# Flamingo cross-attention with a routed FFN: the context of batches 1 to 3 loads as 32-row blocks and is turned by VectorE

## The chip, the core and the metric

The kernel runs on one core of one Trainium2 chip. The metric is the device time of one execution in microseconds (us); three executions of the kernel before took 322.89 to 324.15, with a median of 324.1. The engines are PE (TensorE), ACT (ScalarE), DVE (VectorE), POOL (GpSimd) and SP (SyncE, which here only issues DMAs); "PEld" rows are weight loads of TensorE.

## The reference, cut to what matters

There are 4 batches of 512 tokens with 256 features, 16 heads of 16 features, and attention windows of 64 queries that see their own and the previous 64 keys. Queries come from the normalised x, keys and values from the context.

```python
q = proj(query, W_q, b_q)          # query = layernorm(x)
k = proj(key, W_k, b_k)            # key = value = ctx_1024
v = proj(value, W_v, b_v)
x = _local_attention(q, k, v, mask)
...
x = x + jnp.tanh(g_xattn[0]) * _L0_xattn_ref(_layernorm(x, axis=-1), ctx_1024, ctx_1024, ...)
x = x + jnp.tanh(g_ffn[0]) * _L0_ffn_ref(_layernorm(x, axis=-1), ...)   # top-1 router, 16 experts
```

A projection `proj(x, W, b)` is `x @ W.T + b`, so TensorE needs the context with its features on the partitions (`ctxT`), which is why it has to be transposed.

## The kernel before

The program has an attention part, which works through the four batches one after another, and an expert part, which is the rest of the span. Each engine's order is written out by hand; engines meet only at semaphores. A loop over `b` covers batches 0 to 2; batch 3 (`LAST`) is written out behind it. Iteration `b` also prepares batch `b + 1`, and finishes the projection, the normalisation and the router of batch `b - 1`.

A batch has 16 units: a window and one half of the heads. For a unit, DVE adds the mask to the scores and keeps a minimum (`low_of`, 4 instructions with a small read each), ACT takes the exponent (`exp`, 4 instructions), DVE the reciprocal (`r_total_of`), POOL multiplies (`norm`), PE transposes (`probsT_of`, 4 transposes), and DVE (even units) or ACT (odd units) copies the result out of PSUM (`take_probsT`). `scores(b, c)` makes the scores of four units at once, into banks that `low_of` of the four units before must have read; `attend(b, c)` multiplies four units with v. `project` is the output projection, `x1_of` adds it to x, `route`, `choose`, `count` and `rank_of` are the router.

The context of batch `n` goes through four steps. SP loads it (`load_ctx`, L310) into `ctx_rows`, with token `128 t + p` on partition `p`. PE transposes it in two parts (`ctxT_of`, L1414, 4 transposes each) into the bank `ps_wide`, ACT copies each part into `ctxT` (`take_ctxT`, L696), and PE multiplies: `k_of` (L1435, twice per batch) and `v_of` (L1446). All of this for batch `b + 1` stands in iteration `b`. The bank is shared, so PE waits for ACT's first copy before it writes the second part, and for the second copy before `attend(b, 0)`. Batch 0's context is copied out of PSUM by DVE (L1154).

The order of PE in iteration `b`, from the part that the change touches, is: `v_of(b, 1)`, `ctxT_of(b+1, 0)`, `probsT_of` 4 and 5, `ctxT_of(b+1, 1)`, `xnT_of(b+1, 1)`, `scores(b, 3)`, `attend(b, 0)`, the transposes of x1 of batch `b-1`, `probsT_of` 6 and 7, `q_of(b+1, 0)`, `route(b-1)`, `k_of(b+1, 0)`, `probsT_of` 8 and 9, `attend(b, 1)`, `scores(b+1, 0)`, `probsT_of` 10 and 11 with `count(b-1)`, `project(b, 0)`, `k_of(b+1, 1)`, `q_of(b+1, 1)`. In batch 0 there is no route and no count. `k_of(b+1, 1)` waits for `rank_of`'s first step (L1091) on DVE, because the counts lie in its bank.

SP's order in iteration `b` is `load_ctx(b+1)`, the two shifted copies of v (`shift_v`, each waits for DVE's `take_v`), then loads of the first experts' weights and a store.

Of the kernel before, what the change touches and what calls it, by code (L numbers as in the profile page):

```python
# [27 lines left out]
P = 128  # L28
# [15 lines left out]
def flamingo_kernel(nc, x, ctx_in, mask, g_xattn, g_ffn, W_q, b_q, W_k, b_k, W_v, b_v, W_o, b_o,  # L44
# [25 lines left out]
    with es:  # L70
# [44 lines left out]
        x_all = sb("x_all", [P, B, T, D])  # L115
        ctx_rows = sb("ctx_rows", [P, T, D])
        xn = sb("xn", [P, T, D])
# [93 lines left out]
        xnT_ready, xnT_taken = sem("xnT_ready"), sem("xnT_taken")  # L211
        ctxT_ready, ctxT_taken = sem("ctxT_ready"), sem("ctxT_taken")
        q_ready, q_taken = sem("q_ready"), sem("q_taken")
# [91 lines left out]
        @block.sync  # L305
        def _(sp):
            def load_ctx(n):
                if n > 0:
                    sp.wait_ge(ctxT_ready, value(n - 1, 2, 2))
                sp.dma_start(ctx_rows[:], ctx_in[n].rearrange("(t p) d -> p t d", p=P)).then_inc(ctx_in_s, 16)  # L310

# [35 lines left out]
            load_x(0, T // 2, T, x_in_late)  # L347
            load_ctx(0)
            for i, b in enumerate((b_q, b_k)):
# [11 lines left out]
            for n in range(2, B):  # L361
                load_x(n, 0, T, x_in[n])

            for b in range(B):
                if b < LAST:
                    load_ctx(b + 1)
                shift_v(b, 0)
                if b == LAST:

                    for sent in scattered:  # L370
                        sp.wait_ge(sent, 16 * T)
                    load_rows(0, 0)
                shift_v(b, 1)
                if b == 0:
                    sp.wait_ge(empty_ready, 2)
                    sp.dma_start(queue.rearrange("(s p) c -> p s c", p=P),
                                 empty_row[:].unsqueeze(1).to_broadcast([P, E * CAP // P, ROW])).then_inc(prefilled, 16)
                if 1 <= b <= 2:
                    load_w1(b - 1, b - 1)
                    load_w2(b - 1, b - 1)  # L380
                if b > 0:
                    store_x1(b - 1)
            store_x1(LAST)

# [276 lines left out]
        def _(act):  # L661
# [27 lines left out]

            def take_ctxT(n, k, ps):  # L690
                if not 0 <= n < B:
                    return
                act.wait_ge(ctxT_ready, value(n, 2, k + 1))

                act.wait_ge(v_ready, value(n - 1, 2, 2))
                act.activation(ctxT[:, k], ps[:], ACT.Copy).then_inc(ctxT_taken, 1)  # L696

            def take_k(n, g, ps):
# [94 lines left out]
            for b in range(LAST):  # L793
# [16 lines left out]
                exp(b, 8)  # L810
                take_ctxT(b + 1, 0, ps_wide)
                exp(b, 9)
                take_ctxT(b + 1, 1, ps_wide)
                take_probsT(b, 5)
# [84 lines left out]
        def _(dve):  # L899
# [14 lines left out]
            def x_norm(n):  # L914
# [5 lines left out]
                for t in range(T):  # L920
                    last = dve.tensor_scalar(xn[:, t], x_all[:, n, t], mean_var[:, n, t, 0:1], rstd[:, n, t:t + 1],
                                             ALU.subtract, ALU.mult)
                last.then_inc(xn_ready, 1)

            def mask_set_of(n):
# [246 lines left out]
            for b in range(LAST):  # L1172
# [26 lines left out]
                r_total_of(b, 8)  # L1199
                take_probsT(b, 4)  # L1200
                low_of(b, 12)
                low_of(b, 13)
# [179 lines left out]
        def _(pe):  # L1382
# [4 lines left out]
            def wT_of(i, ps):  # L1387
                pe.wait_ge(w_in[i], 16)
                for k in range(KD):
                    for d in range(KD):  # L1390
                        last = pe.transpose(ps[:, k * D + d * P:k * D + (d + 1) * P],
                                            w_raw[:, i, d, k * P:(k + 1) * P], ident[:])
                last.then_inc(wT_ready, 1)
# [14 lines left out]

            def ctxT_of(n, k, ps):
                if not 0 <= n < B:  # L1410
                    return
                pe.wait_ge(ctx_in_s, 16 * (n + 1))
                for t in range(T):
                    last = pe.transpose(ps[:, t * P:(t + 1) * P], ctx_rows[:, t, k * P:(k + 1) * P], ident[:])  # L1414
                last.then_inc(ctxT_ready, 1)
# [175 lines left out]
            for k in range(KD):  # L1591
                ctxT_of(0, k, bank[k])
            keep_warm(bank[3], 3)
# [11 lines left out]
            for b in range(LAST):  # L1605
# [27 lines left out]
                pe.wait_ge(xnT_taken, value(b + 1, 2, 1))  # L1633
                v_of(b, 1, ps_misc)
                if first:
# [12 lines left out]
                attend(b, 0)  # L1648
# [237 lines left out]
```

## Time and profile before

| what | value |
| --- | --- |
| median of three runs | 324.1 us (322.89 to 324.15) |
| the profiled execution, its own time | 324.57 us |
| its span in the profile | 322.8 us |
| PE, DVE, ACT, POOL busy over the span | 93%, 61%, 55%, 51% |
| granted TensorE clock | 1.00 in all of the span |

A page of the profile shows one execution. Its times are from the span's start. "Busy" of an engine is the union of its instructions; durations of neighbours on DVE and ACT overlap a little, so the distance between two starts is what an instruction costs its engine. In a timeline the brackets at the end of a row tell how long the engine stood idle before it, and who ended that. The busy shares over the span mix two parts: the attention part ends near 168 us, and in the expert part ACT and DVE have little to do.

### The profile page before, as it was taken

How to read it: one execution, taken by the hardware profiler on the slowest of the kernel's cores; microseconds unless marked ns; L12 is line 12 of the kernel's file. 1: busy time of each engine (PE TensorE's matmuls, PEld its weight loads, DVE VectorE, ACT ScalarE, POOL GpSimd, SP SyncE). 2: the span in 40 equal slices, each digit the busy share in tenths (PEclk: the TensorE clock that was granted, in tenths of full speed). 3: DMA queues.
4: the chain of work that ended last, by engine and by line, in shares of the span. 5: the costliest groups of instructions: out<-in, count | busy, mean ns of one | idle time of the engine just before them, and what ended most of it. 6: DMA issues, size and time to landing. Idle time of an engine off the chain costs nothing.

```text
span 322.8 us, 8448 instructions
## 1 busy us (share of the span) xinstructions
PE 299.0 (93%) x2759; PEld 244.6 (76%) x2760; DVE 195.5 (61%) x950; ACT 177.0 (55%) x666; POOL 165.3 (51%) x200
## 2 busy tenths in 40 slices
PE   7868779999999999999897999999999999999994
PEld 3437646887768866777776889898998989898974
DVE  2788898898989879899974232423425161515133
ACT  3379999999999999999754111111110202111110
POOL 6469747789769984989856122131313121121322
PEclk9999999999999999999999999999999999999999
DMA  7921299017512280230324679697979897998900
GB/s 216 288 87 25 61 376 316 7 26 229 197 60 91 58 312 3 87 93 6 95 80 185 164 215 369 201 363 235 367 212 372 238 347 257 306 310 253 365 18 13
DMA packets 48471, 60.55 MB, mean 188 GB/s; under 512 B 14712, under 2 KB 41360, under 8 KB 46384
## 3 DMA queue, kind: packets, MB, share of 16 engines
q1 hardware_dynamic: 44976, 53.20, 51.5%
q0 software_dynamic: 2560, 6.25, 5.3%
q10 hardware_dynamic: 896, 0.61, 0.6%
q8 instruction: 20, 0.33, 0.4%
q14 instruction: 19, 0.16, 0.2%
HBM read 44.60 MB, written 14.19 MB: 182 GB/s over the span
## 4 chain that ended last, share of the span: by engine, by line
PE 58%; ACT 26%; DVE 8%; issue 4%; DMA 1%; POOL 1%; SPq 0%; DVEq 0%; POOLq 0%; ACTq 0%
PE bank L1763 20%; ACT probs L712 18%; PE bank L1788 16%; PE bank L1813 5%; PE bank L1424 3%; ACT probsT L725 3%; DVE probs L958 3%; ACT q_par L686 2%; PE bank L1435 2%; PE bank L1566 1%; DMA x_all<-in_x_dram 1%; PE bank L1774 1%; PE bank L1477 1%; PE bank L1499 1%; PE bank L1537 1%
## 5 line engine op out<-in xcount | busy, mean ns | idle before, releaser
L712 ACT ACTIVATE probs<-probs,low 128x128 f32<-128x128 f32 x256 | 99.4, 407 | 2.2 <-DVE low L958 2.2
L533 POOL TENSOR_TENSOR probs<-probs,r_total 128x512 f32<-128x512 f32 x64 | 66.3, 1046 | 18.1 <-DVE r_total L967 17.6
L1763 PEld LDWEIGHTS bank<-xdT,w 128*128 128x128 f32 x480 | 66.6, 190 | 1.9 <-issue 1.2
L1763 PE MATMUL bank<-xdT,w 128*128 128x160 f32 x480 | 68.0, 300 | 0.0
L958 DVE CUSTOM_DVE_ANT_0 probs<-bank,mask_now 128x128 f32<-128x128 f32 x256 | 57.2, 283 | 6.4 <-PE bank L1465 6.0
L712 ACT ACTIVATION_READ_ACCUMULATOR probs<-probs,low 128x1 f32 x256 | 53.2, 208 | 0.0
L882 ACT ACTIVATE w_raw<-bank 128x480 f32<-128x480 f32 (+1 forms) x24 | 12.4, 526 | 62.7 <-PE bank L1763 35.7
L637 POOL DMA_INDIRECT out_dram<-base,place x16 | 14.0, 874 | 59.2 <-DVE base L1323 37.4
L646 POOL DMA_INDIRECT out_dram<-base,place x16 | 15.7, 979 | 53.7 <-DVE place L1316 43.3
L882 ACT ACTIVATE x_all<-bank 128x480 f32<-128x480 f32 (+1 forms) x24 | 12.6, 526 | 52.2 <-PE bank L1763 32.6
L1333 DVE SCALAR_TENSOR_TENSOR base<-bank,base 128x256 f32<-128x256 f32 x15 | 7.2, 482 | 51.8 <-PE bank L1788 51.8
L1477 PE MATMUL bank<-ident,probs 128*128 128x128 f32 x256 | 35.8, 276 | 2.2 <-DVE probsT L977 1.8
L1323 DVE SCALAR_TENSOR_TENSOR base<-bank,base 32x256 f32<-32x256 f32 x64 | 30.6, 477 | 9.5 <-PE bank L1813 7.6
L1477 PEld LDWEIGHTS bank<-ident,probs 128*128 128x128 f32 x256 | 28.8, 141 | 8.6 <-issue 5.6
L1788 PE MATMUL bank<-w,w_raw 128*128 128x256 f32 x128 | 29.0, 380 | 0.0
L1291 DVE STREAM_TRANSPOSE xdT<-q_blocks 128x320 f32<-128x320 f32 x16 | 8.2, 511 | 32.3 <-DMA q_blocks<-expert_queue 23.5
L1788 PEld LDWEIGHTS bank<-w,w_raw 128*128 128x128 f32 x128 | 23.9, 190 | 3.1 <-issue 0.2
L1788 PE MATMUL bank<-w,x_all 128*128 128x256 f32 x112 | 25.9, 385 | 0.0
L1465 PE MATMUL bank<-kT,q_par 32*128 32x128 f32 x512 | 18.8, 283 | 6.9 <-ACT q_par L686 3.4
L1788 PEld LDWEIGHTS bank<-w,x_all 128*128 128x128 f32 x112 | 20.7, 190 | 5.0 <-issue 2.5
L1465 PEld LDWEIGHTS bank<-kT,q_par 32*128 32x128 f32 x512 | 15.9, 186 | 10.7 <-issue 6.1
L560 POOL DMA_INDIRECT expert_queue<-rows,slot x16 | 16.6, 1036 | 11.4 <-issue 6.9
(147 smaller groups left out, 494.3 us busy)
## 6 DMA issues: line engine op xcount, KB each, us to landing
w<-in_L_ffn_w_dram SPq DMA_DIRECT2D x32, 1024.0 KB, 8.4
expert_queue<-empty_row SPq DMA_DIRECT2D x1, 5140.0 KB, 17.8
q_blocks<-expert_queue SPq DMA_DIRECT2D x62, 40.0 KB
base<-expert_queue SPq DMA_DIRECT2D x16, 129.0 KB
ctx_rows<-in_ctx_dram SPq DMA_DIRECT2D x4, 512.0 KB, 9.3
out_dram<-rows SPq DMA_DIRECT2D x4, 512.0 KB, 6.3
x_all<-in_x_dram SPq DMA_DIRECT2D x3, 512.0 KB, 7.7
v_shift<-v SPq DMA_DIRECT2D x12, 128.0 KB, 2.3
```

What stands on the lines that cost most here:

```text
L533: pool.tensor_tensor(probs[:, i % NP_], probs[:, i % NP_], r_total[:, i % NP_].unsqueeze(2).to_broadcast([P, PAIRS, 2 * WINDOW]), ALU.mult ...
L560: pool.indirect_dma_start(out=queue, out_offset=bass.IndirectOffsetOnAxis(ap=slot[n % 2][:, t:t + 1], axis=0), in_=rows[n % 2][:, t, :], i ...
L646: pool.indirect_dma_start(out=out_rows, out_offset=bass.IndirectOffsetOnAxis(ap=place[i][:, 0:1], axis=0), in_=base[i][:, 0, 0:D], in_offs ...
L712: last = act.activation(probs[:, i % NP_, j], probs[:, i % NP_, j], ACT.Exp, scale=-1.0, bias=low[:, i % NP_, j:j + 1], accum_out=total[:, ...
L882: act.activation(hidden[i][:, ms[0]:ms[-1] + 1, :], ps_hidden[m][:, 0:n].rearrange("p (m c) -> p m c", c=CAP), ACT.Gelu_apprx_tanh).then_i ...
L958: last = dve.tensor_tensor_reduce(probs[:, i % NP_, j], ps_scores[j][:, i % 4 * P:(i % 4 + 1) * P], mask_now[:, w % 2, w // 2], 1.0, 3.0e3 ...
L1323: dve.scalar_tensor_tensor(rest[:, 0:D], ps_rest[i % 2][j * REST:(j + 1) * REST, 0:D], rest[:, D:D + 1], rest[:, 0:D], ALU.mult, ALU.add). ...
L1465: last = pe.matmul(ps_scores[j][:, wi * P:(wi + 1) * P], q_par[rows_j, g, w].rearrange("p e q -> p (e q)"), kT[rows_j, g, w * WINDOW:w * W ...
L1477: last = pe.transpose(ps_probsT[i % 2][:, j * P:(j + 1) * P], probs[:, i % NP_, j], ident[:])
L1763: last = pe.matmul(ps_hidden[m][:, c * CAP:(c + 1) * CAP], w1_sb[i % 2][:, k, f * P:(f + 1) * P], xdT[i % 2][:, k], start=(k == 0), stop=( ...
L1788: last = pe.matmul(ps_y[:, 0:D], hidden[i % 2][:, k, 0:P], w2_sb[i % 2][:, k], start=(k == 0), stop=(k == KF - 1))
L1813: last = pe.matmul(ps_rest[i % 2][j * REST:(j + 1) * REST, 0:D], hidden[i % 2][:, k, P:CAP], w2_sb[i % 2][:, k], start=(step == 0), stop=( ...
```

## The change

From batch 1 on the context is loaded as 32-row blocks: token `32 s + r` lies on partition `32 j + r` for each quarter `j` of the features, with 64 features (256 bytes) in a run. One load becomes four, one for each quarter, each into 32 partitions. DVE's 32 x 32 transposes (`turn_ctx`, two per batch, 128 x 512 elements each) write `ctxT` directly. PE's 8 transposes and ACT's 2 copies per batch are gone for batches 1 to 3. Batch 0 keeps them. Since a turned block has the even features in one half of `ctxT` and the odd in the other, the transposes of W_k and W_v and those of batch 0's context read every second column.

```diff
             def load_ctx(n):
-                if n > 0:
-                    sp.wait_ge(ctxT_ready, value(n - 1, 2, 2))
-                sp.dma_start(ctx_rows[:], ctx_in[n].rearrange("(t p) d -> p t d", p=P)).then_inc(ctx_in_s, 16)
+                if not 0 <= n < B:
+                    return
+                if n == 1:
+                    sp.wait_ge(ctxT_ready, 2)
+                else:
+                    sp.wait_ge(ctxT_turned, value(n - 2, 2, 2))
+                for j in range(P // BLOCK):
+                    sp.dma_start(ctx_blocks[j * BLOCK:(j + 1) * BLOCK],
+                                 ctx_in[n, :, j * KD * BLOCK:(j + 1) * KD * BLOCK].rearrange("(s r) c -> r s c", r=BLOCK)
+                                 ).then_inc(ctx_in_s, 16)
...
-            def take_ctxT(n, k, ps):
...
-                act.activation(ctxT[:, k], ps[:], ACT.Copy).then_inc(ctxT_taken, 1)
...
-                take_ctxT(b + 1, 0, ps_wide)
                 exp(b, 9)
-                take_ctxT(b + 1, 1, ps_wide)
...
+            def turn_ctx(n, half):
+                if not 0 <= n < B:
+                    return
+                dve.wait_ge(ctx_in_s, 16 + 16 * (P // BLOCK) * n)
+
+                dve.wait_ge(v_ready, value(n - 1, 2, 2))
+                blocks = slice(half * (S // BLOCK // 2), (half + 1) * (S // BLOCK // 2))
+                dve.transpose(ctxT[:, :, half * (S // 2):(half + 1) * (S // 2)].rearrange("p k (s r) -> p s k r", r=BLOCK),
+                              ctx_blocks[:, blocks].rearrange("p s (r k) -> p s k r", k=KD)).then_inc(ctxT_turned, 1)
...
                 take_probsT(b, 4)
+                turn_ctx(b + 1, 0)
                 low_of(b, 12)
...
                 take_probsT(b, 6)
+                turn_ctx(b + 1, 1)
                 r_total_of(b, 11)
...
+                        if i in (1, 2):
+
+                            cols = w_raw[:, i, d].rearrange("p (m k) -> p k m", k=KD)[:, k]
...
             def k_of(n, g, ps):
                 if not 0 <= n < B:
                     return
-                pe.wait_ge(ctxT_taken, value(n, 2, 2))
+                if n == 0:
+                    pe.wait_ge(ctxT_taken, 2)
+                else:
+                    pe.wait_ge(ctxT_turned, value(n - 1, 2, 2))
...
-                ctxT_of(b + 1, 0, ps_wide)
-                probsT_of(b, 4)
-                probsT_of(b, 5)
-                pe.wait_ge(ctxT_taken, value(b + 1, 2, 1))
-                ctxT_of(b + 1, 1, ps_wide)
-                pe.wait_ge(v_taken, value(b, 2, 2))
-                xnT_of(b + 1, 1, ps_misc)
-                scores(b, 3)
-                pe.wait_ge(ctxT_taken, value(b + 1, 2, 2))
                 attend(b, 0)
```

On PE, in iteration 0, the stretch from `v_of(0, 1)` (which writes from `ctxT`) to `attend(0, 0)` reads before and after as follows (`ident` is the identity that makes a matmul a transpose, `probs` the softmax, `xn` the normalised x of the next batch):

```order
L1446 MATMUL bank<-wT,ctxT 128x256 x4
L1414 MATMUL bank<-ident,ctx_rows 128x128 x4
L1477 MATMUL bank<-ident,probs 128x128 x8
L1414 MATMUL bank<-ident,ctx_rows 128x128 x4
L1406 MATMUL bank<-ident,xn 128x128 x4
L1465 MATMUL bank<-kT,q_par 128x128 x16
```

```order
L1464 MATMUL bank<-wT,ctxT 128x256 x4
L1495 MATMUL bank<-ident,probs 128x128 x8
L1422 MATMUL bank<-ident,xn 128x128 x4
L1483 MATMUL bank<-kT,q_par 128x128 x16
```

The two groups of four context transposes are gone; `xnT_of` and `scores(0, 3)` stand directly behind the softmax's transposes.

On DVE, in iteration 1, behind `take_att(1, 0)`, the first fence is before and the second after (`r_total` is the reciprocal, `probsT` the copy of unit 6, `probs,low` the masked scores of unit 14):

```order
L921 TENSOR_SCALAR xn<-x_all,mean_var,rstd 128x256 x3
L967 RECIPROCAL r_total<-total 128x4 [waits exp_done]
L977 COPY probsT<-bank 128x512 [waits att_ready,probsT_ready]
L967 RECIPROCAL r_total<-total 128x4 [waits exp_done]
L958 ISA probs,low<-bank,mask_now 128x128 [waits scores_ready,probsT_ready]
```

```order
L922 TENSOR_SCALAR xn<-x_all,mean_var,rstd 128x256 x3
L978 RECIPROCAL r_total<-total 128x4 [waits exp_done]
L988 COPY probsT<-bank 128x512 [waits att_ready,probsT_ready]
L933 STREAM_TRANSPOSE ctxT<-ctx_blocks 128x8x2x32 [waits v_ready,ctx_in]
L978 RECIPROCAL r_total<-total 128x4 [waits exp_done]
L969 ISA probs,low<-bank,mask_now 128x128 [waits scores_ready,probsT_ready]
```

The second turn stands ahead of `r_total_of(1, 11)` and `low_of(1, 14)`, and everything that DVE does for the router follows it. The first turn stands in the same way between `take_probsT(b, 4)` and `low_of(b, 12)`.

On SP, the load of batch 2's context before and after (the row in front of it fills the expert queue with empty rows, 5 MB):

```order
L376 DMA expert_queue<-empty_row 128x20x514 [waits empty_ready]
L310 DMA ctx_rows<-in_ctx_dram 128x4x256 [waits ctxT_ready]
L315 DMA v_shift<-v 64x512 [waits v_taken]
```

```order
L386 DMA expert_queue<-empty_row 128x20x514 [waits empty_ready]
L319 DMA ctx_blocks<-in_ctx_dram 32x16x64 [waits ctxT_turned]
L319 DMA ctx_blocks<-in_ctx_dram 32x16x64 x3
L326 DMA v_shift<-v 64x512 [waits v_taken]
```

The place in SP's queue stays the same; one issue becomes four, and it waits for DVE's second turn instead of PE's second transposes.

## Rows read from the trace of the kernel before

**Rows 1.** Busy PE, PEld, DVE, ACT, POOL by stretch; clock, DMA, GB/s.

```profile
20.00:58.00 38.00, 30.16 (x318) 21.92 (x320) 34.55 (x209) 36.96 (x160) 27.09 (x26) 1.00 0.50 167
58.00:95.00 37.00, 35.71 (x421) 27.64 (x425) 33.39 (x195) 35.85 (x151) 30.72 (x32) 1.00 0.34 107
95.00:131.50 36.50, 35.62 (x423) 27.55 (x419) 31.77 (x191) 35.64 (x153) 29.84 (x30) 1.00 0.35 116
```

**Rows 2.** The chain that ended last, in order of time.

```profile
82.25 0.49 DVE marks L1054
```

**Rows 3.** Groups by form, the removed ones: busy us, mean ns, idle before.

```profile
L1414 PE MATMUL bank<-ident,ctx_rows 128*128 128x128 f32 x32 | 4.8, 278 | 0.0
...
L696 ACT ACTIVATE ctxT<-bank 128x512 f32<-128x512 f32 x6 | 3.5, 590 | 0.5 <-PE bank L1414 0.5
```

**Rows 4.** DVE's turns in the expert part: summary in ns, then timeline.

```profile
L1291 DVE STREAM_TRANSPOSE xdT<-q_blocks x16: 500/511/512, 172.5 to 294.5; 128x320 f32<-128x320 f32 x16
...
206.95 0.51 DVE L1291 STREAM_TRANSPOSE xdT<-q_blocks 128x320 f32<-128x320 f32 x1 [2.56 <-DMA q_blocks<-expert_queue]
207.38 4.03 DVE L1323 SCALAR_TENSOR_TENSOR base<-bank,base 32x256 f32<-32x256 f32 x8
```

**Rows 5.** Timeline of PE, iteration 0: `k_of(1, 0)`, `scores(1, 0)`, `q_of(1, 1)`.

```profile
45.58 1.99 PE L1435 MATMUL bank<-ctxT,wT 128*128 128x512 f32 x4 [1.54 <-ACT q_par L686]
...
49.75 1.17 PE L1465 MATMUL bank<-kT,q_par 32*128 32x128 f32 x32 [0.30 <-issue]
...
55.23 1.88 PE L1424 MATMUL bank<-xnT,wT 128*128 128x512 f32 x4
```

**Rows 6.** Timeline of DVE, iteration 0: `low_of(0, 12)`, `r_total_of(0, 11)`.

```profile
39.91 0.29 DVE L958 CUSTOM_DVE_ANT_0 probs<-bank,mask_now 128x128 f32<-128x128 f32 x1 [1.11 <-PE bank L1465]
...
46.24 0.16 DVE L967 RECIPROCAL r_total<-total 128x4 f32<-128x4 f32 x1
```

**Rows 7.** Timeline of ACT, iteration 0: `take_ctxT(1, 0)` and its successor, `take_q(1, 1)`.

```profile
36.81 0.60 ACT L696 ACTIVATE ctxT<-bank 128x512 f32<-128x512 f32 x1 [0.50 <-PE bank L1414]
37.30 0.39 ACT L712 ACTIVATE probs<-probs,low 128x128 f32<-128x128 f32 x1
...
57.23 1.45 ACT L686 ACTIVATE q_par<-bank,bias_q,scale_q 128x512 f32<-128x512 f32 x2
```

**Rows 8.** Timeline of DVE, iteration 1: `r_total_of(1, 8)`, `low_of(1, 12)`, `choose(0)`.

```profile
73.71 0.17 DVE L967 RECIPROCAL r_total<-total 128x4 f32<-128x4 f32 x1
...
75.47 0.29 DVE L958 CUSTOM_DVE_ANT_0 probs<-bank,mask_now 128x128 f32<-128x128 f32 x1 [1.01 <-PE bank L1465]
...
81.73 0.23 DVE L1049 TENSOR_REDUCE top<-bank 128x4 f32<-128x64 f32 x1 [0.31 <-PE bank L1537]
```

**Rows 9.** Timeline of PE, iteration 1: `scores(1, 3)`, `k_of(2, 1)`.

```profile
74.05 1.17 PE L1465 MATMUL bank<-kT,q_par 32*128 32x128 f32 x32
...
90.30 1.98 PE L1435 MATMUL bank<-ctxT,wT 128*128 128x512 f32 x4 [0.35 <-DVE ranks L1091]
```

**Rows 10.** Timelines of iteration 2: PE's `q_of(3, 0)`, DVE's `choose(1)`.

```profile
114.83 1.98 PE L1424 MATMUL bank<-xnT,wT 128*128 128x512 f32 x4 [0.33 <-ACT x1nT L733]
...
118.54 0.23 DVE L1049 TENSOR_REDUCE top<-bank 128x4 f32<-128x64 f32 x1 [1.07 <-PE bank L1537]
```

**Rows 11.** Summaries of DVE's statistics and normalisation of x, ns min/median/max.

```profile
L907 DVE BATCH_NORM_STATS2 stats<-x_all x16: 401/410/428, 4.4 to 43.6; 128x6 f32<-128x256 f32 x16
...
L921 DVE TENSOR_SCALAR xn<-x_all,mean_var,rstd x16: 379/403/1132, 8.7 to 79.4; 128x256 f32<-128x256 f32 x16
```

**Rows 12.** SP's context loads, batches 1 and 2; time to landing.

```profile
11.78 1.71 SPq L310 DMA_DIRECT2D ctx_rows<-in_ctx_dram  x1
...
39.09 7.86 SPq L310 DMA_DIRECT2D ctx_rows<-in_ctx_dram  x1
...
DMA to landing us min/median/max: 5.9/9.3/18.5
```

**Rows 13.** Timeline of PE at the start: the transposes of batch 0's x.

```profile
10.10 1.09 PE L1406 MATMUL bank<-ident,xn 128*128 128x128 f32 x8 [0.63 <-DVE xn L921]
```

More of the change, by code:

```diff
@@ L115, in flamingo_kernel @@
         x_all = sb("x_all", [P, B, T, D])
-        ctx_rows = sb("ctx_rows", [P, T, D])
+        ctx_blocks = sb("ctx_blocks", [P, S // BLOCK, KD * BLOCK])
+        first_ctx = ctx_blocks[:].rearrange("p s c -> p (s c)").rearrange("p (t d) -> p t d", d=D)
         xn = sb("xn", [P, T, D])
@@ L211, in flamingo_kernel @@
         xnT_ready, xnT_taken = sem("xnT_ready"), sem("xnT_taken")
-        ctxT_ready, ctxT_taken = sem("ctxT_ready"), sem("ctxT_taken")
+        ctxT_ready, ctxT_taken, ctxT_turned = sem("ctxT_ready"), sem("ctxT_taken"), sem("ctxT_turned")
         q_ready, q_taken = sem("q_ready"), sem("q_taken")
@@ L306, in _, with load_first_ctx @@
         def _(sp):
+            def load_first_ctx():
+                sp.dma_start(first_ctx, ctx_in[0].rearrange("(t p) d -> p t d", p=P)).then_inc(ctx_in_s, 16)
             def load_ctx(n):
-                if n > 0:
-                    sp.wait_ge(ctxT_ready, value(n - 1, 2, 2))
-                sp.dma_start(ctx_rows[:], ctx_in[n].rearrange("(t p) d -> p t d", p=P)).then_inc(ctx_in_s, 16)
+                if not 0 <= n < B:
[8 more added lines that the diff above has]
+                                 ).then_inc(ctx_in_s, 16)
             def shift_v(n, m):
@@ L347, in _ @@
             load_x(0, T // 2, T, x_in_late)
-            load_ctx(0)
+            load_first_ctx()
             for i, b in enumerate((b_q, b_k)):
@@ L362, in _ @@
                 load_x(n, 0, T, x_in[n])
+            load_ctx(1)
             for b in range(B):
-                if b < LAST:
-                    load_ctx(b + 1)
                 shift_v(b, 0)
@@ L382, in _ @@
                     store_x1(b - 1)
+                load_ctx(b + 2)
             store_x1(LAST)
@@ L688, in take_q @@
                 last.then_inc(q_taken, 1)
-            def take_ctxT(n, k, ps):
[L691 to L695, printed above, removed]
-                act.activation(ctxT[:, k], ps[:], ACT.Copy).then_inc(ctxT_taken, 1)
             def take_k(n, g, ps):
@@ L1390, in wT_of @@
                     for d in range(KD):
-                        last = pe.transpose(ps[:, k * D + d * P:k * D + (d + 1) * P],
-                                            w_raw[:, i, d, k * P:(k + 1) * P], ident[:])
+                        cols = w_raw[:, i, d, k * P:(k + 1) * P]
+                        if i in (1, 2):
+                            cols = w_raw[:, i, d].rearrange("p (m k) -> p k m", k=KD)[:, k]
+                        last = pe.transpose(ps[:, k * D + d * P:k * D + (d + 1) * P], cols, ident[:])
                 last.then_inc(wT_ready, 1)
@@ L1407, in xnT_of, with first_ctxT_of @@
                 last.then_inc(xnT_ready, 1)
[L1409 to L1412, printed above, removed]
+            def first_ctxT_of(k, ps):
+                pe.wait_ge(ctx_in_s, 16)
                 for t in range(T):
-                    last = pe.transpose(ps[:, t * P:(t + 1) * P], ctx_rows[:, t, k * P:(k + 1) * P], ident[:])
+                    last = pe.transpose(ps[:, t * P:(t + 1) * P],
+                                        first_ctx[:, t].rearrange("p (m k) -> p k m", k=KD)[:, k], ident[:])
                 last.then_inc(ctxT_ready, 1)
@@ L1591, in _ @@
             for k in range(KD):
-                ctxT_of(0, k, bank[k])
+                first_ctxT_of(k, bank[k])
             keep_warm(bank[3], 3)
@@ L1634, in _ @@
                 v_of(b, 1, ps_misc)
+                probsT_of(b, 4)
+                probsT_of(b, 5)
+                pe.wait_ge(v_taken, value(b, 2, 2))
+                xnT_of(b + 1, 1, ps_misc)
+                scores(b, 3)
                 if first:
```

## The prediction, made before the changed kernel ran

> **What bounds the kernel now.** I read the busy times by stretch first, because the shares over the whole span hide the attention part. In iterations 0 to 2 ACT is busy 36.96 of 38.00, 35.85 of 37.00 and 35.64 of 36.50 us, and PE 35.71 and 35.62 us in the last two: both are within 1.4 us of full. DVE is busy 33.39 and 31.77 us there, so it has 3.6 to 4.7 us to spare [rows 1]. On that count a move from ACT and PE to DVE looks free. The chain that ended last says otherwise: in iteration 1 it is on DVE at 82.25, in the router, and on PE at 90.30, where `k_of` waited for DVE's ranks [rows 2, 9]. DVE has slack over an iteration, but none in its second half. The clock is full throughout [rows 1], and the expert part is not touched, so the sum is that of three iterations; what they end earlier or later the last batch and the experts inherit, since nothing in them is changed.
>
> **What is removed.** ACT loses 6 copies with a busy time of 590 ns [rows 3]; neighbours overlap, and a copy holds ACT 0.49 us (36.81 to 37.30), after an idle of 0.50 us in iteration 0 [rows 7], which is all the idle in front of the six [rows 3]. Together 6 x 0.49 + 0.5 = 3.4 us of ACT. PE loses 24 of its 32 context transposes. Their 278 ns [rows 3] are mostly pipeline: the 32 are busy 4.8 us together, 0.15 each at most, so 24 are 2.6 to 3.6 us, 0.44 us being my value per four. If ACT's time came back in full, the kernel would gain 3.4 us.
>
> **What is added on DVE.** No turn of 128 x 512 is in the trace; the nearest is 128 x 320, busy 511 ns, the next instruction starting 0.43 us after it (206.95 to 207.38) [rows 4]. From below, if further elements were free, one turn holds DVE for 0.43 us; from above, if the whole busy time grew with the elements, for 511 x 512/320 = 818 ns. I take the middle, 0.63, which is 1 ns for each of the 192 further elements. Six turns are 3.8 us.
>
> **Where it lies, iteration 0.** `scores(b, 3)` must wait for `low_of(b, 11)`, which ends where `r_total_of(b, 8)` starts: 73.71, against a start of the scores at 74.05 [rows 8, 9]. So with the context transposes away the scores start only 0.3 us earlier (I use this for every iteration), and `low_of(b, 12)` too. The first turn fills the hole of 1.01 to 1.11 us that DVE had there [rows 6, 8]: the hole less 0.3 is 0.7 to 0.8, the turn 0.63. It costs nothing; without that hole it would cost its 0.63. The second turn has no hole. `take_probsT(0, 6)` ended at 46.24 [rows 6], now 45.94, so the turn ends at 46.57. `k_of(1, 0)` needs it, and started at 45.58, held by ACT's q [rows 5]. ACT could now release it earlier, but the turn holds it until 46.6: 1.0 us late. Behind it on PE stand two unit transposes, `attend`, `scores(1, 0)`, `project`, `k_of` and `q_of(1, 1)`, with one idle of 0.30 us [rows 5], so `q_of(1, 1)` starts 1.0 - 0.3 = 0.7 us late. Before it started at 55.23 and ACT took q at 57.23 [rows 5, 7], 2.0 us later, which is one `q_of`: ACT had no slack here. So everything ACT gained in iteration 0 (some 1.5 us) is lost, and all engines go on **+0.7 us** late.
>
> **Iteration 1.** ACT is the bound until `q_of(2, 0)`, and saves two copies. But DVE, late by 0.7, gains 0.3 at `low_of(1, 12)`: +0.4. The second turn adds 0.63, the idle of 0.31 us in front of `choose(0)` [rows 8] takes 0.31 of it: +0.7. From `choose` to `rank_of` DVE has no idle of that kind, and `k_of(2, 1)` waited for the ranks [rows 9]. All go on **+0.7 us**: the iteration itself costs 0.0, ACT's saving is absorbed again.
>
> **Iteration 2.** There is no x to normalise, so DVE has room: 1.07 us idle before `choose(1)` [rows 10] hides the second turn. PE decides: `scores(2, 3)` is at 0.7 - 0.3 = +0.4, and `q_of(3, 0)`, which had stood 0.33 us waiting for ACT's copy of x1 [rows 10], now waits for its own queue instead: ACT's copy comes earlier, 0.33 and some 0.1 of pipeline overlap go. +0.4 - 0.4 = **0.0**. Batch 3 starts where it did.
>
> **Edits that I cost at nothing.** Strided reads: the transposes of W_k (4) and of batch 0's context (8) stand ahead of PE's wait of 0.63 us for the normalised x at 10.10 [rows 13]; that wait is their cover. If they took twice their 0.11 us, 12 x 0.11 - 0.63 = 0.7 us would show, and 0.4 more for W_v's four behind it. Loads: the four issues stand in the same place of SP's queue. Batch 1's go out from 11.78 and are used near 39; the slowest load before took 18.5 us to land, behind the 5 MB fill. Batch 2's was issued at 39.09 behind that fill [rows 12]; it now waits for the turn that ends at 46.6, still behind the fill, and is used at 75. Batch 3's waits for iteration 1's second turn and has an iteration's time. Behind each on SP stands only `shift_v`, which waits for v long after.
>
> **Sum.** +0.7 + 0.0 - 0.7 = 0.0 us on the profiled execution's 324.57 (span 322.8). The median of the runs is 324.1, 0.5 lower; my time is **324.1 us**. The second turns of iterations 0 and 1 lie on the path: with 0.43 per turn the sum is 2 x 0.2 less, -0.4, with 0.82 it is +0.4. The gap to 3.4 us is the point: the work leaves two full engines, but the wait it ends on moves to DVE.
>
> **Rivals.** *ACT's time comes back* (chance 0.23). For it speaks that ACT is 97% busy [rows 1]. Against it: `q_of(1, 1)` and the ranks. If the DVE-bound halves have more give than their printed idles show, 2.0 to 3.4 us come back: 321.0 to 322.1. *The turns stall behind POOL* (0.17). The normalisation of x, SBUF to SBUF on DVE, takes 403 ns in the median but up to 1132 [rows 11], so DVE can be held some 0.7 us by POOL's work; the statistics, SBUF too, stay at 401 to 428. If each turn is held as long, the first of an iteration takes 1.3 us in a hole of 0.75 (+0.6) and the second is 0.7 longer: +1.3 in each of iterations 0 and 1, while 2 has room. That is 326.7, or 325.4 if half are held; I take 326.0. It decides once a first turn takes over 0.75 us. [...] *Batch 1's load is late* (0.05): four issues into 32 partitions each, in short runs, may land late. At twice the slowest load, 37 us from 11.78, they land at 49 against a use at 39, and DVE and all behind it stand for 10 us: 334. It decides from a landing time of 27 us; the 18.5 was behind 5 MB, which batch 1's load is not. [...] *Little moves at all*, since ACT's copies were cover for PE, is the forecast itself by another road.
>
> **How the numbers follow.** Forecast, 324.1, own range 322.9 to 325.3: 0.55. With the three rivals, 1.0. For 8 in 10 the range leaves out the late load and the outer half of ACT's return and of the stall: 321.7 to 326.0. A measurement here tells 0.5% (1.6 us) from no change. Faster than 322.5: ACT's return plus a tail of the forecast, 0.27; slower than 325.7: the stall, the late load and a little of the forecast's tail, 0.22; within: 0.51.
>
> **What would show it.** Turns: six rows of about 0.71 us on DVE, 0.63 to the next start. `k_of(1, 0)` near 46.6 with its idle ended by DVE's `ctxT`, not by ACT. ACT idle before `take_q(1, 1)` (0.6 to 0.8 us) and `take_q(2, 1)`. `k_of(2, 1)` near 91.0, still ended by the ranks. Context loads landed before 39. It is wrong if ACT stays near 97% busy in all three iterations and the part ends earlier, if turns are over 0.8 us, or if a turn waits for a DMA.

## The result, and the profile after it

The changed kernel takes **327.44 us** in the median of six runs (326.02 to 329.06); the kernel before took 324.11 us in six runs (322.89 to 326.64). The ratio is 1.0116, with a 95% interval of 1.0081 to 1.0151: slower by 3.3 us in the medians and by 3.8 us (2.6 to 4.9) by the ratio. Three executions of the kernel before, made beside the experiments (328.87, 332.73 and 333.19 us), were in a slower state and stand in no median and no ratio below. The forecast was 324.1, its range 321.7 to 326.0. The profiled execution of the changed kernel took 329.06 us, with a span of 327.2 us and a mean granted clock of 0.982. So it is 1.6 us above its own median, and the one before was 0.5 above its own: of the 4.4 us between the two spans not all belongs to the change.

The kernel's lines moved: `k_of` is L1453 (before L1435), `q_of` L1439, `scores` L1483, `attend` L1517, `probsT_of` L1495, the turn L933, the context load L319. The first view of the changed kernel is the page's busy shares in 40 slices of 8.2 us, here PE and the granted clock:

```profile
PE   7869759999999998999899999989999999999994
...
PEclk9997977999999999999999999999999999999999
```

The clock is the first difference from before, where every digit of this row was 9. It is at 7 tenths in slices 3, 5 and 6 (counted from 0), which are 25 to 33 and 41 to 57 us. The same in stretches, to be read beside [rows 1] (busy us and count of PE, PEld, DVE, ACT, POOL, then clock, DMA share, GB/s). The kernel is 3.5 us late from the middle of iteration 0 on, so the last two stretches begin that much earlier in the work than those of [rows 1]:

```profile
41.00:58.00 17.00, 13.57 (x103) 8.73 (x102) 12.20 (x62) 12.78 (x54) 9.10 (x9) 0.80 0.99 309
...
20.00:58.00 38.00, 29.91 (x292) 21.66 (x291) 31.92 (x184) 33.41 (x147) 25.34 (x24) 0.87 0.57 171
58.00:95.00 37.00, 35.05 (x407) 26.71 (x406) 34.54 (x197) 35.07 (x150) 29.62 (x30) 1.00 0.37 100
95.00:131.50 36.50, 34.78 (x407) 26.68 (x406) 33.38 (x193) 34.44 (x147) 29.70 (x29) 1.00 0.37 115
```

In stretches of half a microsecond the granted clock of this execution is 1.00 or 0.50, with a value between them only where it changes; it is 0.50 from 46.0 to 52.5 us. So a mean of 0.80 over 17 us means that 6.8 us of it ran at 0.50. Two more things are to be seen. ACT fell to 33.41 us in iteration 0, 3.6 below [rows 1], much of it because it stood and waited. And in iterations 1 and 2 ACT is 0.8 and 1.2 us less busy than before, near the 2 x 0.49 us of its two copies, while DVE is busy 1.2 and 1.6 us more, near the two turns.

Where iteration 0 lost its time stands in PE's timeline of the changed kernel (start, us, engine, line, operation, count, and in brackets the idle time before with what ended it):

```profile
41.23 1.88 PE L1439 MATMUL bank<-xnT,wT 128*128 128x512 f32 x4
46.54 3.75 PE L1453 MATMUL bank<-ctxT,wT 128*128 128x512 f32 x4 [3.43 <-DVE ctxT L933]
50.09 1.91 PE L1495 MATMUL bank<-ident,probs 128*128 128x128 f32 x8
51.93 0.66 PE L1517 MATMUL bank<-probsT,v_shift 128*32 128x128 f32 x8
52.36 0.51 PE L1517 MATMUL bank<-probsT,v 128*32 128x128 f32 x8
52.70 0.39 PE L1517 MATMUL bank<-probsT,v_shift 128*32 128x128 f32 x8
52.91 0.39 PE L1517 MATMUL bank<-probsT,v 128*32 128x128 f32 x8
53.23 1.17 PE L1483 MATMUL bank<-kT,q_par 32*128 32x128 f32 x32
```

`k_of(1, 0)` starts at 46.54, 1.0 us later than in [rows 5], released by the second turn after 3.43 us of idle time. But then its four matmuls take 3.75 us where they took 1.99, and the eight unit transposes behind it 1.91 where such eights take 1.04; in the middle of `attend` the rows are back at 0.39. `scores(1, 0)` is at 53.23 against 49.75: 3.5 us late. The turn itself, in its summary and in DVE's timeline around the second one:

```profile
L933 DVE STREAM_TRANSPOSE ctxT<-ctx_blocks x6: 689/698/702, 38.4 to 119.1; 128x512 f32<-128x512 f32 x6
...
  PE bank L1453: 3.6, 2
```

```profile
45.70 0.70 DVE L933 STREAM_TRANSPOSE ctxT<-ctx_blocks 128x512 f32<-128x512 f32 x1
46.33 0.13 DVE L978 RECIPROCAL r_total<-total 128x4 f32<-128x4 f32 x1
```

All six turns take 689 to 702 ns. The second turns, which have work right behind them, hold DVE for 0.63 us (45.70 to 46.33), the value that the prediction took.

Iterations 1 and 2 pass the lateness on. `k_of(2, 1)` is at 93.89 (before 90.30), `k_of(3, 1)` at 130.38 (before 126.70, with no idle time in front of it), now both released by the ranks. In iteration 2 DVE's timeline shows why nothing came back (the router's first rows; between the two quoted pieces stands `low_of(2, 15)` and what follows it), and under it PE's `k_of(3, 1)`:

```profile
121.50 0.22 DVE L1060 TENSOR_REDUCE top<-bank 128x4 f32<-128x64 f32 x1 [0.84 <-PE bank L1555]
121.76 0.22 DVE L1062 TENSOR_TENSOR lowered<-bank,top 128x64 f32<-128x64 f32 x1
122.01 1.19 DVE L1065 SCALAR_TENSOR_TENSOR marks<-lowered,countdown 128x64 f32<-128x64 f32 x1
123.12 0.21 DVE L1069 TENSOR_TENSOR scaled<-lowered,rstd 128x64 f32<-128x64 f32 x1
...
130.11 0.21 DVE L1102 TENSOR_TENSOR ranks<-bank,onehot 128x64 f32<-128x64 f32 x1
```

```profile
130.38 1.98 PE L1453 MATMUL bank<-ctxT,wT 128*128 128x512 f32 x4 [0.44 <-DVE ranks L1102]
```

`choose(1)` began 2.96 us later than before (121.50 against 118.54, [rows 10]), so 0.6 us had been won by then. The row `marks` then took 1.19 us, where before it took 0.56, and the ranks came 3.68 us late.

### The profile page after: what moved, and what is told of

It is laid out like the page before. It is cut to its first block, busy times and chain, and to the rows that moved or that the text cites. A ratio compares the mean times of both kernels' runs of the same rounds, so it can differ in the third digit from the quotient of the medians.

```text
span 327.2 us, 8403 instructions
## 1 busy us (share of the span) xinstructions
PE 301.2 (92%) x2735; PEld 244.5 (75%) x2736; DVE 199.5 (61%) x956; ACT 174.6 (53%) x660; POOL 165.3 (51%) x200
## 4 chain that ended last, share of the span: by engine, by line
PE 62%; DVE 15%; ACT 12%; DMA 5%; issue 5%; POOL 1%; SPq 1%; DVEq 0%; POOLq 0%; ACTq 0%
PE bank L1777 19%; PE bank L1802 14%; ACT probs L715 10%; DVE probs L969 5%; PE bank L1827 4%; PE bank L1495 4%; PE bank L1453 3%; PE bank L1483 3%; PE bank L1517 3%; PE bank L1531 2%; PE bank L1439 2%; DMA w<-in_L_ffn_w_dram 2%; DMA out_dram<-base,place 2%; DVE probsT L988 1%; PE bank L1788 1%
## 5 line engine op out<-in xcount | busy, mean ns | idle before, releaser
L715 ACT ACTIVATION_READ_ACCUMULATOR probs<-probs,low 128x1 f32 x256 | 51.7, 202 | 0.0
L883 ACT ACTIVATE x_all<-bank 128x480 f32<-128x480 f32 (+1 forms) x24 | 12.6, 526 | 52.5 <-PE bank L1777 52.5
L1495 PE MATMUL bank<-ident,probs 128*128 128x128 f32 x256 | 37.0, 282 | 2.4 <-DVE probsT L988 1.9
L1495 PEld LDWEIGHTS bank<-ident,probs 128*128 128x128 f32 x256 | 30.0, 145 | 9.8 <-issue 7.0
L1483 PE MATMUL bank<-kT,q_par 32*128 32x128 f32 x512 | 18.8, 282 | 6.5 <-ACT q_par L697 3.4
L1483 PEld LDWEIGHTS bank<-kT,q_par 32*128 32x128 f32 x512 | 15.9, 186 | 10.3 <-issue 5.8
```

Of the source, the lines that this page charges most:

```text
L715: last = act.activation(probs[:, i % NP_, j], probs[:, i % NP_, j], ACT.Exp, scale=-1.0, bias=low[:, i % NP_, j:j + 1], accum_out=total[:, ...
L883: act.activation(hidden[i][:, ms[0]:ms[-1] + 1, :], ps_hidden[m][:, 0:n].rearrange("p (m c) -> p m c", c=CAP), ACT.Gelu_apprx_tanh).then_i ...
L1483: last = pe.matmul(ps_scores[j][:, wi * P:(wi + 1) * P], q_par[rows_j, g, w].rearrange("p e q -> p (e q)"), kT[rows_j, g, w * WINDOW:w * W ...
L1495: last = pe.transpose(ps_probsT[i % 2][:, j * P:(j + 1) * P], probs[:, i % NP_, j], ident[:])
```

## The experiments

Each kernel ran beside the kernel before on the same chip; a ratio is against the runs of before made beside it, whose medians were 323.64 us for e1 to e4 (35 runs), 323.79 for e5 to e8 (22) and 324.04 for e9 to e11 (16). It is not the quotient of the two medians and can lie 0.1 to 0.2% from it (e10: 1.0091, and 1.0108 by the medians). 0.1% is 0.32 us. Each kernel has one profile. The thirteen profiles do not begin alike: `scores(0, 1)`, which stands ahead of every turn, starts between 23.57 and 24.43 us (24.14 before, 23.81 in the changed kernel), an offset that is there already at PE's first transposes of x (9.52 to 10.38). Where a few tenths matter, the distance from `scores(0, 1)` is given. The **clock theory** says that the idle time which the second turn makes on PE brings the clock down, and that this costs more than the wait. The **queue theory** says that the turns' 3.8 us on DVE cost what they cost wherever they stand. e1 to e4 were to tell these apart.

**e1: both turns together.** The second turn goes up behind the first in every iteration.

```diff
                 turn_ctx(b + 1, 0)
+                turn_ctx(b + 1, 1)
                 low_of(b, 12)
...
                 take_probsT(b, 6)
-                turn_ctx(b + 1, 1)
```

> The changed kernel with each second turn moved up behind the first, so that VectorE has turned the whole next context at about 40.0 us instead of 46.3. Clock theory (the second turn holds TensorE idle for 3.43 us in front of k_of(1, 0), the granted clock falls, and the fall costs some 2.8 of the 3.3 us): k_of(1, 0) is released by ScalarE's q again near 45.5, the idle in front of it is 2 to 3 us, the row of k_of(1, 0) is 2.0 us and not 3.75, and the median is 324.5 (323.5 to 325.5). Queue theory (the six turns cost VectorE their 0.63 us each wherever they stand, the clock is incidental): 327 us, as the low masks of unit 12 start 0.3 to 0.6 us later in every iteration.

Measured: 323.94 us, ratio 1.0010 (0.9988 to 1.0032). PE's timeline of this kernel, the same place:

```profile
44.90 1.98 PE L1453 MATMUL bank<-ctxT,wT 128*128 128x512 f32 x4 [1.54 <-ACT q_par L697]
...
49.07 1.17 PE L1483 MATMUL bank<-kT,q_par 32*128 32x128 f32 x32 [0.31 <-issue]
```

`k_of(1, 0)` is released by ACT's q again, with the very 1.54 us of [rows 5], and at 1.98 us. The six turns are all still there; their place made the loss.

**e2: idle matmuls in the gap.** The changed kernel, in iteration 0 only:

```diff
+                if first:
+                    pe.wait_ge(att_taken, value(b, 4, 1))
+                    keep_warm(ps_wide, 14)
                 pe.wait_ge(q_taken, value(b + 1, 2, 1))
                 k_of(b + 1, 0, ps_misc)
```

> The changed kernel with 14 idle matmuls of 512 columns (bf16, zeros, about 0.2 us each) in front of k_of(1, 0) in iteration 0 alone, once the bank is free; they fill the 3.43 us in which TensorE stood idle, and k_of(1, 0) starts where it did, at 46.5. Clock theory: the granted clock stays at its full level from 41 to 58 us, the row of k_of(1, 0) is 2.0 us, scores(1, 0) are at 50.5 instead of 53.23, and the median is 324.8 (324.0 to 325.5). Queue theory: nothing changes, 327.4.

Measured: 325.95 us, ratio 1.0060 (1.0039 to 1.0082). The timeline of PE and, under it, the stretch that stood at 0.80:

```profile
43.34 2.97 PE L1398 MATMUL bank<-idle_rows 128*128 128x512 bf16 x13
46.73 1.96 PE L1453 MATMUL bank<-ctxT,wT 128*128 128x512 f32 x4 [0.42 <-DVE ctxT L933]
...
50.50 1.17 PE L1483 MATMUL bank<-kT,q_par 32*128 32x128 f32 x32
```

```profile
41.00:58.00 17.00, 16.53 (x126) 9.99 (x125) 14.96 (x82) 14.91 (x64) 10.16 (x10) 1.00 1.00 313
```

`k_of(1, 0)` is held as long as in the changed kernel (22.73 us behind `scores(0, 1)` in both), the granted clock stays at 1.00, and `scores(1, 0)` are at 50.50: 0.75 us after the kernel before, 0.9 by the distance from `scores(0, 1)`, close to where the prediction had put them (+0.7). The median is 1.5 us under the changed kernel's; by the ratios it is 1.8, give or take 1.3. But it is 1.1 above what was expected, outside the expected range; that rest comes back below. That the clock stayed up is shown for the profiled execution alone; two of the twelve runs have a mean clock of 0.988.

**e3: the wait without the turns.** The kernel before, `k_of(1, 0)` held by one more wait:

```diff
+                if first:
+                    pe.wait_ge(r_total_ready, value(b, UNITS, 12))
                 pe.wait_ge(q_taken, value(b + 1, 2, 1))
                 k_of(b + 1, 0, ps_misc)
```

> The kernel before, with one wait more: k_of(1, 0) waits until VectorE has done r_total_of(0, 11), near 46.5 us, where the changed kernel's second turn ends; no turn, no other load, no strided read. Clock theory: TensorE stands idle for 2.5 to 3 us, the clock falls as in the changed kernel, and the median is 326.5 to 327.5. If only the wait itself costs: k_of(1, 0) is 0.9 us late, of which 0.3 is taken up by an idle behind it: 324.7. Queue theory: no turns, so 324.1 to 324.7.

Measured: 325.06 us, ratio 1.0053 (1.0027 to 1.0079), twelve runs from 323.38 to 327.88. This lies between the two theories (326.5 or more, 324.7) and decides nothing. The profiled execution, at 323.38 the fastest of the twelve, shows an idle time of 2.42 us, a granted clock of 1.00 from 41 to 58 us and `k_of` at 1.98 us; the hold was shorter than the changed kernel's 3.43 us, and the runs scattered more than those of e1, e2 and e4. It was repeated with a longer hold as e7.

**e4: the turns without the wait.** The kernel before, with `dve.transpose` of 128 x 512 from `wT[:, 1]` into a spare tile:

```diff
                 take_probsT(b, 4)
+                turn_spare(b + 1, 0)
                 low_of(b, 12)
...
                 take_probsT(b, 6)
+                turn_spare(b + 1, 1)
```

> The kernel before with six turns of 128 x 512 added on VectorE in the places of the changed kernel, from a fixed tile into a spare one that nobody reads: VectorE's load of the change alone, with TensorE's and ScalarE's work as before and nobody waiting for a turn. Clock theory: k_of(1, 0) is released by ScalarE's q at 45.6 as before, the clock stays full, and only what VectorE is late by in iterations 0 and 1 shows: 324.1 to 325.3. Queue theory: the six turns cost what they cost in the changed kernel: 327.4 or more, as ScalarE and TensorE have not been relieved.

Measured: 324.37 us, ratio 1.0012 (0.9997 to 1.0028). DVE's load alone costs 0.4 us, at most 0.9 and perhaps nothing; the queue theory, which had asked for 327.4, falls.

**e5: the changed kernel again**, beside e6 to e8.

> The changed kernel itself once more, on the same chip as the three others here. Theory so far, out of three parts: the second turn of iteration 0 holds k_of(1, 0) back (0.9 us), the clock falls during that idle time in about half of the runs (1.7 us of work each time), and something of 0.5 to 1 us in the experts. So: 326.8 to 327.5 in the median, and the runs fall into two groups, one with a mean clock of 0.993 or more near 326.3 and one of 0.984 or less near 328.2. If the clock has no part in it, there are no two groups and the time doesn't follow the clock.

Measured: 327.86 us, ratio 1.0110 (1.0072 to 1.0149). Its profile repeats the step, with another amount of it:

```profile
47.28 2.44 PE L1453 MATMUL bank<-ctxT,wT 128*128 128x512 f32 x4 [3.44 <-DVE ctxT L933]
49.51 1.91 PE L1495 MATMUL bank<-ident,probs 128*128 128x128 f32 x8
...
52.66 1.17 PE L1483 MATMUL bank<-kT,q_par 32*128 32x128 f32 x32
```

```profile
41.00:58.00 17.00, 13.56 (x110) 9.18 (x109) 13.47 (x72) 13.95 (x60) 9.10 (x9) 0.90 1.03 325
```

0.90 over 17 us is 3.4 us at a granted clock of 0.50 instead of 6.8. The "two groups" of the expectation are not borne out: the six times are spread from 324.95 to 328.87, and the run at the mean clock of 0.991 is the fastest. The mean clock of a whole run is a poor guide, since it also counts a low clock when PE has finished (in this profile at 322.2 of 326.4 us, with 0.50 from 325.2 on), or near 25 us (0.50 from 24.8 to 28.1), where it cost little (last section).

**e6: the second turn early in iteration 0 only.**

```diff
                 turn_ctx(b + 1, 0)
+                if b == 0:
+                    turn_ctx(b + 1, 1)
...
-                turn_ctx(b + 1, 1)
+                if b > 0:
+                    turn_ctx(b + 1, 1)
```

> The changed kernel with the second turn moved up behind the first in iteration 0 only; in iterations 1 and 2 it stays in front of r_total_of(b, 11). Theory (the loss is made in iteration 0, where k_of(1, 0) waits for the turn and the clock falls): as with both turns together everywhere, 324.0 (323.3 to 324.7). Rival (the second turns of iterations 1 and 2 hold VectorE in front of the router and cost 0.3 to 0.6 us each): 325.0 or more.

Measured: 323.67 us, ratio 1.0000 (0.9980 to 1.0021). The loss hangs on the place of one instruction, executed once.

**e7: the wait without the turns, as long as the changed kernel's.**

```diff
+                if first:
+                    pe.wait_ge(scores_taken, value(b, UNITS, 15))
                 pe.wait_ge(q_taken, value(b + 1, 2, 1))
                 k_of(b + 1, 0, ps_misc)
```

> The kernel before, with k_of(1, 0) held until VectorE has done low_of(0, 14), near 47.3 us: TensorE's idle time in front of it is 3.4 us, that of the changed kernel, with no turn in the program. k_of(1, 0) is 1.7 us late, of which 0.3 is taken up behind it, so a wait alone costs 1.4 us: 325.1. Clock theory: the clock falls in this idle time in most runs and half speed costs up to 1.7 us more of work: 326.5 to 327, with the slow ones at a mean clock of 0.99 or less.

Measured: 326.41 us, ratio 1.0085 (1.0053 to 1.0117). That is at the lower edge of the clock theory's range and 1.3 above the wait's own price. Its timeline has the changed kernel's step with no turn in the program, and the granted clock has a mean of 0.90 from 41 to 58 us, as in e5:

```profile
47.26 3.14 PE L1435 MATMUL bank<-ctxT,wT 128*128 128x512 f32 x4 [3.24 <-DVE low L958]
...
52.74 1.17 PE L1465 MATMUL bank<-kT,q_par 32*128 32x128 f32 x32
```

**e11: the same wait, with idle matmuls in the gap.** It is e7 with two lines more:

```diff
                 if first:
+                    pe.wait_ge(att_taken, value(b, 4, 1))
+                    keep_warm(ps_wide, 14)
                     pe.wait_ge(scores_taken, value(b, UNITS, 15))
```

> The kernel before with k_of(1, 0) held until 47.3 us, as in the run of that name (326.41), and 14 idle matmuls in the 3.4 us in front of it. Clock theory: the wait alone is left, 1.7 - 0.3 = 1.4 us, 325.0 (324.6 to 325.5), k_of(1, 0)'s row is 2.0 us, and no run has the lower clock in this place. If the clock has no part: 326.4.

Measured: 325.63 us, ratio 1.0042 (1.0029 to 1.0055):

```profile
43.58 3.19 PE L1385 MATMUL bank<-idle_rows 128*128 128x512 bf16 x14
46.99 1.98 PE L1435 MATMUL bank<-ctxT,wT 128*128 128x512 f32 x4 [0.22 <-DVE low L958]
...
50.79 1.17 PE L1465 MATMUL bank<-kT,q_par 32*128 32x128 f32 x32
```

0.42% is 1.4 us, the worked-out price of the wait alone (the median itself is 0.1 above the expected range); e7's 0.85% is 2.75 us. The granted clock is 1.00 from 41 to 58 us here, against 0.90 in e7: the clock is the other 1.4 us, give or take 1.1; by the medians it is 1.0. By my estimate from the clock rows, 3.4 us at 0.50 do 1.7 us less work, which lies within that.

The profiles show the price without the scatter of the runs. From the start of `k_of(1, 0)` to that of `scores(1, 0)` PE does the same work in all these kernels. At a granted clock of 1.00 it took 3.77 us (e2) and 3.80 (e11); it took 5.48 in e7, 5.38 in e5, 5.46 in e10 below (46.67 to 52.13), and 6.69 in the first profile of the changed kernel. So the lower clock cost 1.6 to 1.7 us where it lasted 3.4 us, and 2.9 us where it lasted 6.8. Each is near half the time at 0.50: half of 3.4 us is 1.7, and of the 6.8 us in the first profile 0.8 fell into the idle time, where they cost nothing, so that 3.0 is half of the rest.

**e8: DVE relieved by ACT.** Both turns together as in e1, and ACT takes the even halves of two attention groups.

```diff
                 exp(b, 10)
+                take_even_att(b, 0)
                 take_x1nT_or_gate(b - 1, ps_misc)
...
                 take_probsT(b, 9)
+                take_even_att(b, 1)
...
-                take_att(b, 0)
+                take_att(b, 0, False)
...
-                take_att(b, 1)
+                take_att(b, 1, False)
```

> Both turns together behind take_probsT(b, 4), and ScalarE, relieved of the context copies, takes the even halves of attention groups 0 and 1 (0.49 us each on VectorE) in iterations 0 to 2. With both turns together VectorE had no idle from 76 to 93 us, and k_of(2, 1) waited 0.67 us for its ranks. If VectorE's load in the router's stretch is what eats ScalarE's saving: the ranks come 0.5 to 0.8 us earlier, TensorE's wait for them goes, and each of iterations 1 and 2 gains 0.3 to 0.7 us: 322.6 (322.0 to 323.2). If TensorE or ScalarE bound it anyway: 323.9, as with the turns together.

Measured: 323.33 us, ratio 0.9997 (0.9982 to 1.0013): no gain to be told. In its profile the last scores of batch 3 are at 146.2 us, against 147.0 in e1 and 147.5 in the kernel before, so the attention part did get shorter than e1's, by 0.8 us, or by 0.7 from `scores(0, 1)`. The experts' part then took 0.8 us longer (170.9 against 170.1 us from the last scores to PE's last matmul). PE's wait for the ranks, 0.67 us in e1, is 0.44 here:

```profile
88.95 1.55 PE L1456 MATMUL bank<-ctxT,wT 128*128 128x512 f32 x3 [0.44 <-DVE ranks L1105]
```

**e9 and e10: the loads.** The rest that e2 left seemed to lie in the experts: from the last scores to PE's last matmul the changed kernel took 171.9 us, e2 171.5 and e5 171.6, where e3, e7 and e1 took 169.7, 170.1 and 170.1. (The trace of the kernel before, with 171.2, already spoke against a common cause in the turned kernels.) Rows such as this one of the changed kernel stood there (the waits by engine, line and what was waited for):

```profile
PE bank L1777 <- DMA w<-in_L_ffn_w_dram: 1.5, 1, 1.5
```

So the loads were exchanged. e9 is the kernel before with the block loads, behind the same wait:

```diff
...
-                sp.dma_start(ctx_rows[:], ctx_in[n].rearrange("(t p) d -> p t d", p=P)).then_inc(ctx_in_s, 16)
+                for j in range(P // BLOCK):
+                    sp.dma_start(blocks[j * BLOCK:(j + 1) * BLOCK],
+                                 ctx_in[n, :, j * KD * BLOCK:(j + 1) * KD * BLOCK].rearrange("(s r) c -> r s c", r=BLOCK)
+                                 ).then_inc(ctx_in_s, 16)
...
```

and e10 the changed kernel with one whole load, the same lines the other way round. In both, the elements of these contexts then stand in another order than the rest of the program expects, so the result is not the right one; the amount of work is the same.

> The kernel before, with the contexts of batches 1 to 3 loaded as the changed kernel does (four issues of 32 partitions, 256-byte runs), in the place where the whole load stood; the matmul transposes then read the context of these batches in another order of elements, so that part of the result is left wrong. The experts' part took 0.5 to 1.5 us more in every profile of the changed kernel's family than in those of the kernel before with other waits. Loads theory: it comes with the block loads, so this kernel takes 324.3 to 325 against 323.7. Otherwise: 323.7, and the experts' part from the last scores to TensorE's last matmul is 169.7 to 170.7 us as before.

> The changed kernel with each context of batches 1 to 3 loaded whole by one issue, rows in order, into the same bytes, and turned as before; what is turned is then in another order of elements, so that the context's part of the result is left wrong. Loads theory: the weights of experts 2 and 3 land earlier, the experts' part falls from 171.5 to about 170.3 us, and the median is 326.2 to 326.6. Otherwise: 327.4 to 327.9 as the changed kernel.

Measured: e9 324.22 us, ratio 0.9998 (0.9981 to 1.0015), e10 327.54 us, ratio 1.0091 (1.0059 to 1.0123). The loads theory falls both ways: the block loads cost the kernel before nothing that shows, and the changed kernel without them is as slow as with them (1.0110 and 1.0116, within the intervals). e9's experts' part was 171.3 us and e10's 171.8, as if nothing had been exchanged.

## Why the prediction was wrong, point by point

**The step that failed** is "Where it lies, iteration 0", with the sentence on which it stood: "The clock is full throughout", carried over from the trace of before to a kernel in which PE waits longer. The step named the right wait, the right releaser and the right moment, and priced it as a delay only: 1.0 us late, less an idle of 0.30. The prediction worked out when `k_of(1, 0)` would start, but not how long PE would then have stood: 3.4 us. What the runs showed in its place: around the end of that idle time the granted clock went from 1.00 to 0.50, for 3.4 us (e5) or 6.8 us (the first profile), and `scores(1, 0)` came 3.5 us late instead of 0.7. With the gap filled (e2) they come 0.75 us late. On the time, filling the gap took 1.5 us off in e2 and 1.0 to 1.4 us between e7 and e11.

**Right.** The turn's price: 0.63 us predicted and measured. That the middle between two bounds, 0.43 and 0.82, was met to the hundredth is luck. No turn was held by POOL: each of the six ran beside a row of POOL, as the second one, from 45.70 on, beside one from 45.28 to 46.32, and all took 689 to 702 ns. `k_of(1, 0)`: 46.57 predicted, 46.54 measured, its idle ended by DVE's `ctxT`. The releaser was right; the last tenths are luck. This execution was 0.33 us ahead at `scores(0, 1)` already, the scores gained some 0.2 us where 0.3 was forecast, and `k_of` starts 0.84 us behind the start of the turn, not 0.63. From `scores(0, 1)` it is 1.3 us late (22.73 against 21.44), not 1.0. The first turn hides in DVE's hole: `low_of(0, 12)` started at 39.37 behind 0.27 us of idle, against 39.91 in [rows 6]. Iteration 1 costs about nothing by itself: `k_of(1, 1)` was 3.5 us late (57.00 against 53.51), `k_of(2, 1)` 3.6 us, still released by the ranks. At a granted clock of 1.00, in e2, `k_of(2, 1)` was at 91.2 against a forecast near 91.0. ACT stood idle 0.80 us before `take_q(1, 1)` (60.63), forecast 0.6 to 0.8. The context loads landed in 4.4 to 9.4 us, where the whole ones took 5.9 to 18.5 [rows 12], and no turn waited for one.

**Wrong by size: iteration 2.** It was to give back 0.7 us and gave back nothing in any profile. Up to `choose(1)` it did: `q_of(3, 0)` did not wait, and 0.6 us were won. What the step left out is that `k_of(3, 1)`, too, stands behind the ranks once PE is earlier, and that DVE's `marks` took 1.19 us instead of 0.56. In e2, with a granted clock of 1.00 from 20 to 131.5 us, `k_of(3, 1)` is at 127.64 against 126.70: +0.9, where the forecast had 0.0. So even without the clock the forecast would have been about 0.9 us low (1.1 from `scores(0, 1)`). In all seven profiles in which the context is turned for use `marks` took 1.17 to 1.20 us, in the six others 0.56 to 0.60.

**The rivals.** The stall behind POOL (326.0) was nearest in time and did not happen; the turns' rows show it. The row on which it stood, the 1132 ns of [rows 11], ran in the trace of before from 21.80 on beside a row of POOL from 21.66 to 22.78, and DVE's next one started at 22.85. The late load did not happen. ACT's time did not come back: e1, e6 and e8, in which nothing is lost in front of `k_of(1, 0)`, come out at 1.0010, 1.0000 and 0.9997. So the gist of the forecast, that 3.4 us taken off ACT buy nothing, holds once the second turn stands earlier. Its reason, that the waits move to DVE, is supported (in e1 both `k_of(2, 1)` and `k_of(3, 1)` wait for the ranks, 0.67 and 0.44 us, against 0.35 and none before; in e8 the attention part got shorter with DVE relieved), but no run turned it into time. This rival's own sum has a slip: 2.0 to 3.4 us off 324.1 is 320.7 to 322.1, not 321.0 to 322.1.

**What stays open.** Of the 1.9 us by which e2 exceeds the kernel before, its attention part shows 0.9 (last scores at 148.4 against 147.5). Where the rest lies is not shown. The experts' part varies from 169.7 to 171.9 us among the thirteen profiles, for different reasons: a weight load awaited for 1.5 us in one, 1.5 us before an expert's first product in another. The four kernels with the late turn had 171.5 to 171.9, the nine others 169.7 to 171.3. But the trace of the kernel before itself has 171.2, so against it this part explains 0.3 us of e2's rest and 0.7 of the changed kernel's 4.4 in the spans. The exchange of loads did not explain it; with one profile each, chance is not excluded, and no cause is shown. Nor was it shown why the clock stayed low for 6.8 us in one execution and for 3.4 in the others.

## What to carry to other kernels

When a change makes an engine wait longer, work out the whole idle time in front of the released instruction, not only by how much it is late, and ask for TensorE what the clock does behind it. Between e7 and e11 the clock cost about as much as the delay itself (1.4 us each); in the first profile of the changed kernel it cost four times as much (3.5 us late instead of 0.7). If work is moved from a full engine to one that is nearly full, put it where the trace shows a hole, ahead of what the other engines wait for, even if it seems early and is longer than the hole (here both turns in front of `low_of(b, 12)`).

## What the runs showed of the hardware that was not expected

The clock after an idle time of PE is not the same in every execution. In front of `k_of(1, 0)` an idle of 1.54 us never brought it down in the profiles, one of 2.42 us did not in the single profile of it, and those of 3.24 to 3.44 us did in all four. It did not fall at a fixed point of the work: in stretches of half a microsecond the lower level begins 0.8 us before PE resumes in the first profile of the changed kernel, and 0.6, 0.7 and 1.3 us after PE has resumed in e10, e7 and e5. At the start of iteration 0 one and the same idle time (2.69 us before `scores(0, 1)`, 2.70 in e2) was followed by a stretch at 0.50 in ten of the thirteen profiles and not in the others: the mean clock from 20 to 41 us was 0.92 in the ten, and 1.00 before, in e2 and in e9. The work there does not decide it, since e3 and e7 have in this stretch the work of the kernel before. It cost little: from `scores(0, 1)` to the held `k_of(1, 0)` it is 22.73 us in the first profile of the changed kernel, with that stretch, and 22.73 in e2, without it; in e5 and e10, with it, 22.85 and 23.08.

DVE's `marks` lasted until an instruction of POOL had ended: in iterations 1 and 2 of all thirteen profiles the DVE instruction behind `marks` started within 0.02 us of such an end. The timelines of POOL of the kernel before and of the changed one, where they touch it in iteration 2:

```profile
117.50 2.02 POOL L533 TENSOR_TENSOR probs<-probs,r_total 128x512 f32<-128x512 f32 x2
```

```profile
121.09 2.03 POOL L544 TENSOR_TENSOR probs<-probs,r_total 128x512 f32<-128x512 f32 x2
```

POOL's pair ended at 119.52 and 123.12, and the instruction behind `marks` started at 119.54 and 123.12. By moving 0.6 us against POOL, the same row became 0.63 us longer; in e1 a `marks` in iteration 1 took 0.34 us, from 81.30 on, and POOL's pair ended at 81.56.
